# Attention output with its layer norm tile by tile, its weights loaded in the prologue, and the last feed-forward chunk moved into the tail block

## The reference

```python
x = _layernorm(x + _L0_attn_ref(x, ...))   # 16 heads of 64, full 2048x2048 softmax, rope; out @ out_w + out_b
x = _layernorm(x + _L0_ffn_ref(x, ...))    # two layers: windowed attention (8 heads, window 64) + GEGLU
x = _layernorm(x + _L1_attn_ref(x, ...))   # rwkv: five token-shift mixes, a decaying scan over the tokens, gate
x = _layernorm(x + _L1_ffn_ref(x, ...))    # silu(x @ wg) * (x @ wu) @ wd, weights given as integers
```

```python
return out @ out_w + out_b                     # end of _L0_attn_ref
def _layernorm(x): return (x - mean(x)) / sqrt(var(x) + 1e-5)
# end of each of the two layers of _L0_ffn_ref (HID = 341):
h = shift_token(x); h = (h - mu) / sqrt(var + 1e-5) * lg + lb
h = h @ w1 + b1
a, g = split(h, 2);  h = a * gelu(g, exact)
x = x + h @ w2 + b2
# the scan of _L1_attn_ref
S = exp(w_t)[..., None] * S + k_t[..., :, None] * v_t[..., None, :]
```

## Time and profile before

| | us |
|---|---|
| median of 3 runs | 1880.84 (1878.97 to 1882.34) |
| profiled execution | 1881.02 |
| span of the profiled execution | 1879.2 |
| mean granted TensorE clock | 0.971 of full speed |
| heads end, attention output begins | 1234.3 |
| next block after the norm (`local_layers`) begins | 1295.9 |
| first instruction of `phase_tail` | 1691.6 |

### The profile page before, as it was taken

The page is one execution under the profiler, slowest core; times in us unless marked ns, Lnnn a source line. Parts: engine busy times, 40 slices in busy tenths (PEclk is TensorE's granted clock), DMA queues, the critical chain, the costliest instruction groups (busy, mean ns, idle before and its releaser), DMA issues. The chain is left out here.

```text
span 1879.2 us, 54358 instructions
## 1 busy us (share of the span) xinstructions
PE 1753.0 (93%) x23048; PEld 1111.1 (59%) x23048; DVE 1409.3 (75%) x2595; ACT 1417.4 (75%) x1780; POOL 1426.3 (76%) x846
## 2 busy tenths in 40 slices
PE   5899999999999999999999999985899999977997
PEld 2466666666666666666666666674556666653454
DVE  5778778787878778787878776425988888844785
ACT  1688888888888888888888889922898888843463
POOL 3599999999998998999999999974765666624122
PEclk8899999999999999999999999987999999997988
DMA  4011010101111010101111010050211111100000
GB/s 121 24 25 31 19 31 22 28 23 30 24 25 27 22 31 19 31 23 26 27 26 27 19 27 2 2 174 12 44 42 36 36 37 40 34 7 13 0 1 23
DMA packets 71082, 56.91 MB, mean 30 GB/s; under 512 B 29197, under 2 KB 64185, under 8 KB 70841
## 3 DMA queue, kind: packets, MB, share of 16 engines
q1 hardware_dynamic: 70840, 53.44, 11.3%
HBM read 14.54 MB, written 1.05 MB: 8 GB/s over the span
## 5 line engine op out<-in xcount | busy, mean ns | idle before, releaser
L294 POOL TENSOR_TENSOR ah_probs_lo<-ah_probs,ah_probs_hi 128x1024 f16<-128x1024 f32 x512 | 1074.8, 2135 | 107.1 <-ACT ah_probs L493 104.8
L550 DVE TENSOR_REDUCE ah_part_max<-ah_p_m 128x1 f32<-128x512 f32 x1024 | 666.8, 684 | 165.4 <-PE ah_p_m L358 156.0
L490 ACT ACTIVATE ah_probs_hi<-ah_p_s 128x1024 f16<-128x1024 f32 x512 | 529.0, 1033 | 183.3 <-PE ah_p_s L377 177.4
L493 ACT ACTIVATE ah_probs<-ah_p_s 128x1024 f32<-128x1024 f32 x512 | 529.8, 1035 | 0.0
L391 PE MATMUL ah_p_o<-ah_v_hi,ah_probs_hi 128*128 128x65 f16 x4096 | 470.6, 195 | 4.9 <-POOL ah_probs_lo L294 4.7
L393 PE MATMUL ah_p_o<-ah_v_lo,ah_probs_hi 128*128 128x64 f16 x4096 | 470.5, 193 | 0.0
L395 PE MATMUL ah_p_o<-ah_v_hi,ah_probs_lo 128*128 128x65 f16 x4096 | 470.3, 194 | 0.0
L391 PEld LDWEIGHTS ah_p_o<-ah_v_hi,ah_probs_hi 128*128 128x128 f16 x4096 | 383.1, 98 | 86.0 <-DVE a_attn L565 12.2
L393 PEld LDWEIGHTS ah_p_o<-ah_v_lo,ah_probs_hi 128*128 128x128 f16 x4096 | 378.5, 98 | 91.5
L358 PE MATMUL ah_p_m<-ah_k_hi_lo,ah_q_hi_twice 128*128 128x512 f16 x1024 | 393.9, 385 | 7.0 <-DVE ah_part_max L550 5.5
L376 PE MATMUL ah_p_s<-ah_q_hi_twice,ah_k_hi_lo 128*128 128x512 f16 x1024 | 388.7, 380 | 1.1 <-ACT ah_probs L493 0.9
(11 more groups left out here) (291 smaller groups left out, 3096.1 us busy)
## 6 DMA issues: line engine op xcount, KB each, us to landing
ba_v_skew<-ba_v_own SPq DMA_DIRECT2D x64, 129.0 KB, 2.3
ah_q_hi_twice<-ah_hi SPq DMA_DIRECT2D x128, 64.0 KB, 2.0
ah_k_hi_lo<-ah_hi SPq DMA_DIRECT2D x64, 64.0 KB, 1.9
ah_one_k_hi<-ah_hi SPq DMA_DIRECT2D x64, 64.0 KB, 2.0
ah_k_hi_lo<-ah_lo SPq DMA_DIRECT2D x64, 64.0 KB, 2.0
ah_max_q_lo<-ah_lo SPq DMA_DIRECT2D x64, 64.0 KB, 2.0
ah_w_head<-in_w_heads SPq DMA_DIRECT2D x16, 160.0 KB, 2.4
bw_rot<-in_rot SPq DMA_DIRECT2D x4, 512.0 KB, 9.9
```

The costliest lines, as they stand in the source:

```text
L294: pool.tensor_tensor(pl[:, p % RW, :, :], pb[:, p % RP, :, :], ph[:, p % RW, :, :], ALU.subtract).then_inc(lo_pool, 1)
L490: act.activation(ph[:, p % RW, :, :], p_s[:, p % 2, :, :], ACT.Exp, scale=HD ** -0.5)
L493: act.activation(pb[:, p % RP, :, :], p_s[:, p % 2, :, :], ACT.Exp, scale=HD ** -0.5).then_inc(exp_done, 1)
L550: dve.tensor_reduce(part[:, t, 2 * half + b:2 * half + b + 1], p_m[:, b, :], AX, ALU.max).then_inc(maxed, 1)
```

## The change

It has three parts.

**Attention output.** `wo`, the output bias and the value bias are loaded in the prologue of `mha_heads`, behind the weights of head 1. There PE multiplies the value bias with `wo` (eight products between two pieces of the prologue), DVE adds the output bias, and POOL adds the result to x in place before its loop. In `mha_out` nothing is left of this path. The row is written back into x, and its statistics and aggregate follow on DVE at once. Of each group of four tiles the root (ACT), the reciprocal and shift (DVE) and the norms (all on ACT, four tiles) are done during the next group; the last group's follow the last tile. `layernorm_block` is gone. `wqkv` is held only for this block.

**Last chunk.** `w1`, `w2`, `b1` and `h2T` are kept over the end of `local_layers`, whose pipeline now ends three steps earlier, after the last `h2T`. In `phase_tail` PE begins with the six products, then `turn_x(0)`, the twelve products back, and `turn_x(1)`. ACT has the three gelus ahead of `norm(0, 0)`, DVE the three multiplications between the statistics of chunks 0 and 1, and the residual behind `delta_z(0)`.

**Scan state.** The state is kept in two chunk buffers per head instead of four, with a copy of one column after the scan in the first three chunks.

```diff
@@ mha_heads: SP, POOL, PE, DVE
+                sp.dma_start(bo[:, :, :], a["b_o"]).then_inc(wo_in, 16)
+                sp.dma_start(bv[:, :], a["b_v"]).then_inc(wo_in, 16)
+                sp.dma_start(wo[:, :, :], a["wo_a"].rearrange("(c p) d -> p c d", p=P)).then_inc(wo_in, 16)
...
+                pool.wait_ge(x_turned, NCH)
+                pool.wait_ge(bias_done, 1)
+                pool.tensor_tensor(x_sb[:, :, :], x_sb[:, :, :], bias[:, :, :].to_broadcast([P, NT, D]),
+                                   ALU.add).then_inc(biased, 1)
...
+                pe.wait_ge(wo_in, 3 * 16)
+                for c in range(IC):
+                    mm = pe.matmul(p_a[:, 0:D], bv[:, c:c + 1].to_broadcast([P, P]), wo[:, c, :], start=(c == 0),
+                                   stop=(c == IC - 1))
+                mm.then_inc(bias_turned, 1)
                 early_v(LEAD_G - 2)
                 for q in range(PAIRS_A):
                     maxima(q)
+                pe.wait_ge(bias_done, 1)
                 turn_max(0)
...
                 low(LEAD_G - 2)
+                dve.wait_ge(bias_turned, 1)
+                dve.tensor_tensor(bias[:, 0, :], p_a[:, 0:D], bo[:, 0, :], ALU.add).then_inc(bias_done, 1)
                 low_v(LEAD_G - 2)
@@ mha_out: ACT, POOL, DVE
+                def root(g):
+                    act.wait_ge(var_done, TPC * (g + 1))
+                    act.activation(std[:, g * TPC:(g + 1) * TPC], mv[:, g * TPC:(g + 1) * TPC, 1], ACT.Sqrt,
+                                   bias=eps[:, 0:1]).then_inc(std_done, 1)
+
+                def norm(g):
+                    act.wait_ge(shift_done, g + 1)
+                    for t in range(g * TPC, (g + 1) * TPC):
+                        act.activation(x_sb[:, t, :], x_sb[:, t, :], ACT.Identity, scale=rstd[:, t:t + 1],
+                                       bias=shift[:, t:t + 1]).then_inc(normed, 1)
+
+                act.wait_ge(eps_set, 1)
+                act.activation(std[:, 0:1], eps[:, :], ACT.Sqrt).then_inc(table_in, 1)
+                act.wait_ge(table_in, 1)
                 for t in range(NT):
                     act.wait_ge(turned, t + 1)
                     if t >= 2:
                         act.wait_ge(y_ready, t - 1)
                     act.activation(aT[:, t % 2, 0:4, :], p_t[:, t % 2, 0, :].rearrange("p (c t) -> p c t", t=P),
                                    ACT.Copy).then_inc(copied_a, 1)
+                    g, i = divmod(t, TPC)
+                    if i == 2 and g >= 1:
+                        root(g - 1)
+                    if i == 3 and g >= 1:
+                        norm(g - 1)
+                root(NT // TPC - 1)
+                norm(NT // TPC - 1)
 
             @block.gpsimd
             def _(pool):
-                pool.wait_ge(w_in, 48)
-                pool.tensor_copy(bvw[:, :, :], bv[:, :].unsqueeze(2).to_broadcast([P, IC, P])).then_inc(widened, 1)
-                pool.wait_ge(bias_done, 1)
-                pool.tensor_tensor(xb[:, :, :], x_sb[:, :, :], bias[:, :, :].to_broadcast([P, NT, D]),
-                                   ALU.add).then_inc(biased, 1)
                 local.prepare(pool)
 
             @block.vector
             def _(dve):
+                def row(t):
+                    dve.wait_ge(y_ready, t + 1)
+                    dve.tensor_tensor(x_sb[:, t, :], p_y[:, t % 2, 0:D], x_sb[:, t, :], ALU.add).then_inc(rows_ready, 1)
+                    dve.wait_ge(rows_ready, t + 1)
+                    dve.bn_stats(stats[:, t, :], x_sb[:, t, :]).then_inc(stats_done, 1)
+                    dve.wait_ge(stats_done, t + 1)
+                    dve.bn_aggr(mv[:, t, :], stats[:, t, :]).then_inc(var_done, 1)
+
+                def shifts(g):
+                    ts = slice(g * TPC, (g + 1) * TPC)
+                    dve.wait_ge(std_done, g + 1)
+                    dve.reciprocal(rstd[:, ts], std[:, ts]).then_inc(rstd_done, 1)
+                    dve.wait_ge(rstd_done, g + 1)
+                    dve.scalar_tensor_tensor(shift[:, ts], mv[:, ts, 0], -1.0, rstd[:, ts], ALU.mult,
+                                             ALU.mult).then_inc(shift_done, 1)
+
+                dve.memset(eps[:, :], LN_EPS).then_inc(eps_set, 1)
                 for t in range(NT):
-                    if t == 1:
-                        dve.wait_ge(bias_turned, 1)
-                        dve.tensor_tensor(bias[:, 0, :], p_b[:, 0:D], bo[:, 0, :], ALU.add).then_inc(bias_done, 1)
                     dve.wait_ge(turned, t + 1)
                     if t >= 2:
                         dve.wait_ge(y_ready, t - 1)
                     dve.tensor_copy(aT[:, t % 2, 4:8, :],
                                     p_t[:, t % 2, 1, :].rearrange("p (c t) -> p c t", t=P)).then_inc(copied_b, 1)
-                    if t == 1:
-                        dve.wait_ge(biased, 1)
                     if t >= 1:
-                        dve.wait_ge(y_ready, t)
-                        dve.tensor_tensor(rows[:, t - 1, :], p_y[:, (t - 1) % 2, 0:D], xb[:, t - 1, :],
-                                          ALU.add).then_inc(rows_ready, 1)
-                dve.wait_ge(y_ready, NT)
-                dve.tensor_tensor(rows[:, NT - 1, :], p_y[:, (NT - 1) % 2, 0:D], xb[:, NT - 1, :],
-                                  ALU.add).then_inc(rows_ready, 1)
-        layernorm_block(nc, ln, "aln_", rows, x_sb)
+                        row(t - 1)
+                    g, i = divmod(t, TPC)
+                    if i == 3 and g >= 1:
+                        shifts(g - 1)
+                row(NT - 1)
+                shifts(NT // TPC - 1)
@@ local_layers
-STEPS_B = TILES + FIRST_G - 1
+STEPS_B = TILES + 6
...
-            return (m, r) if 0 <= m < CHUNKS else (m, -1)
+            return (m, r) if 0 <= m < CHUNKS - 1 else (m, -1)
@@ phase_tail: PE, ACT, POOL, DVE
+                        if n == 1:
+                            pe.wait_ge(lres_done, 1)
...
+                def last_products():
+                    for banks, col, ready in ((last_gate, lw.hid, lgate_ready), (last_value, 0, lvalue_ready)):
+                        for k, (first_row, n) in enumerate(chunks):
+                            cs = slice(col + first_row, col + first_row + n)
+                            pe.matmul(banks[k][0:n, :], lw.w1[:, DEPTH - 1, cs], lw.hT2[:, 1, :], start=True,
+                                      stop=True).then_inc(ready, 1)
+
+                def last_down():
+                    pe.wait_ge(lhidden, len(chunks))
+                    for t in range(TPC):
+                        for k, (first_row, n) in enumerate(chunks):
+                            n += k == len(chunks) - 1
+                            mm = pe.matmul(p_kr[:, 1, t * P:(t + 1) * P], hT[0:n, 1, k, t * P:(t + 1) * P],
+                                           lw.w2[0:n, DEPTH - 1, k, :], start=(k == 0), stop=(k == len(chunks) - 1))
+                    mm.then_inc(ldown_ready, 1)
+
+                last_products()
                 turn_x(0)
+                last_down()
                 turn_x(1)
...
+                for k, (first_row, n) in enumerate(chunks):
+                    act.wait_ge(lgate_ready, k + 1)
+                    act.activation(hT[0:n, 0, k, :], last_gate[k][0:n, :], ACT.Gelu,
+                                   bias=lw.b1[0:n, DEPTH - 1, 1, k:k + 1]).then_inc(gelu_done, 1)
                 norm(0, 0)
...
+                pool.memset(hT[:, 1, HC - 1, :], 1.0).then_inc(ones_set, 1)
                 pool.memset(neg_half[:, :], -0.5).then_inc(cleared, 1)
-                pool.memset(st[:, :, 0:1], 0.0).then_inc(cleared, 1)
+                pool.memset(st[:, :, 0, 0:1], 0.0).then_inc(cleared, 1)
...
                 dve.memset(xTp[:, 0:1], 0.0).then_inc(zeroed, 1)
+                dve.wait_ge(ones_set, 1)
+                for k, (first_row, n) in enumerate(chunks):
+                    dve.wait_ge(gelu_done, k + 1)
+                    dve.wait_ge(lvalue_ready, k + 1)
+                    dve.scalar_tensor_tensor(hT[0:n, 1, k, :], last_value[k][0:n, :],
+                                             lw.b1[0:n, DEPTH - 1, 0, k:k + 1], hT[0:n, 0, k, :], ALU.add,
+                                             ALU.mult).then_inc(lhidden, 1)
                 ln_stats(0, 1)
...
                 delta_z(0)
+                dve.wait_ge(ldown_ready, 1)
+                dve.tensor_tensor(x_sb[:, tiles(CLAST), :], each(p_kr[:, 1, :]), x_sb[:, tiles(CLAST), :],
+                                  ALU.add).then_inc(lres_done, 1)
                 ln_stats(0, 2)
                 delta_z(1)
...
                     if c == 0:
+                        dve.wait_ge(lres_done, 1)
                         ln_stats(0, CLAST)
...
-                        dve.wait_ge(scanned, n - HCH + 1)
-                    dve.tensor_tensor_scan(st[:, h, xtok(c)], dec[:, n % 2, :], kv[:, n % 2, :],
-                                           st[:, h, c * CH:c * CH + 1], ALU.mult, ALU.add).then_inc(scanned, 1)
```

(5 more changed lines are left out.)

117 lines of the change are left out of this document (37 added, 80 removed).

## The result

The changed kernel takes 1860.66 us (median of 5 runs, 1856.94 to 1865.37), the kernel before on the same chip 1882.06: ratio 0.9893, 95% interval 0.9876 to 0.9910. The medians differ by 21.4 us, the ratio stands for 20; 22.2 were forecast and the range held. The two profiled executions differ by 20.3 us of span (1879.2 and 1858.9), and milestones read from the timelines say where. Each is the start of an instruction: a turn, the last row's addition on VectorE, the first eight records of a `mixes` on PE, the last scan.

What follows compares the result with a forecast made beforehand. PE was taken as busy 93% of the span, so gains come only where it waits: attention output 10.9 plus last chunk 11.6 less scan state 0.3 is 22.2 us off 1881.02, giving 1858.8; range 1854.0 to 1867.0.

Steps and rivals of the forecast that it cites:

- Attention output, front: Start of attention output: without the bias path, turn 2 starts at about 1240.0 instead of 1246.88, gaining 6.9 us.
- Attention output, middle: Attention output's tiles: pitch stays 2.66 us, but shifts wait beside POOL's preparation, costing 1.0 us, bounds 0 and 3.
- a few tenths: Attention output, middle: room left for ACT's norms making the copy behind them late, given a slack of 0.1 us.
- the slack of 0.1 a group: Attention output, middle: ACT's copy behind the norms done about 3.4 us after PE's turns, asked for at 3.5.
- Attention output, end: After the last row's start: last norm ends after 3.5 us instead of 8.54, gaining 5.0, bounds 4.3 and 5.4.
- Prologue and carry: Heads' prologue: loads and bias work cost nothing, bounds -0.5 and +1; scan state's column copies: 0.3 us, bounds 0 and 1.8.
- Last chunk: Tail start: six products begin at 1679.9, mixes(0) at 1697.9 instead of 1707.53; gain 11.6 us by mixes(1).
- it stays: Tail: PE's clock stays full through the 2.0 to 2.2 us idle before turn_x(1); if it falls, gain 7.3.
- the first rival: Tail: the clock falls in the gap, last chunk gains 7.3 us instead of 11.6, time 1863.1; chance 0.28.
- DVE or ACT holds PE: Attention output: DVE steps wait for POOL or ACT's norms delay copies, 5.5 us in all, time 1864.3; chance 0.09.
- The slower case: Heads: new loads or bias path upset them, PE waiting longer for wo or turns losing 0.35 us; 1885 us; chance 0.04.

Runs made afterwards that it cites:

- filling: Changed kernel with extra identity transposes in PE's waits: last stage alone 1859.7 us; heads' end, last local turn, tail and last stage 1853.55 us.
- the one-input form: Changed kernel with each group's shift computed by four 128x1 instructions with one tensor input each, instead of one with two: 1860.68 us, ratio 0.9891.

## Why the prediction was right, point by point

The range held and the order of the waits was right. That the forecast came so close is in part luck: the moved parts gave 18.1 us, where 22.2 were forecast, and 2.2 came from stages that had been put at nothing.

- *Attention output, front* (6.9): 6.6. The clock came back 5 us after the start, as taken over from the bias product. That it is half at the start is not the block's doing but comes from short waits of PE at the heads' end, which I had not looked at; filling them brings 2.0 more.
- *Attention output, middle* (-1.0, bounds 0 and 3): -1.8 in the profile of the changed kernel, and -1.0 to -5.0 in the others of that form. The mechanism was right and its size too small: I took half an instruction of POOL for each of a group's two instructions. The reciprocal never waited (0.14 to 0.15), and the shift waited to the end of POOL's first, second or third. The bound of 3 was passed in two profiles, in one of them with 1.6 us of half clock. The share of ScalarE, "a few tenths", is 0.24: the slack of 0.1 a group was a lack of 0.12.
- *Attention output, end* (5.0): 5.3. The bounds for this whole part were added up wrongly: 8 to 12.5 is stated, its terms give 7.2 to 12.3. The measured 10.1 lies in both.
- *Prologue and carry* (0 and -0.3): 0 and -0.18, shown by the kernels that have the one without the other.
- *Last chunk* (11.6): 8.9 up to mixes(0), where 9.6 was forecast; the order of waits was right to the half microsecond. Of the missing 0.7, most is the six products: their pace of before was taken over, 7.0 us, and with more of them at half clock they took 8.0. The step that failed is the clock. I asked only whether it would fall in the gap ahead of turn_x(1), and took "it stays" from a wait of 2.41 us that had done no harm. It did stay there, and fell after the following gap of 2.22 us, when PE was at work again, and again after one of 2.53. That cost 1.3 to 1.4 in each of two `mixes` and left a gain of 8.1, between the forecast and the first rival's 7.3. Whether it falls is not a property of the code: the kernel with the last chunk alone ran the same mixes(1) at full pace (8.39 to mixes(2), 9.71 in the changed kernel). One difference is 0.2 off in the prediction: 13.5 less 2.2 is 11.3 and not 11.5; with a full clock 11.50 was measured.
- *What I left out*: the stages whose code doesn't change moved by -1.3 (local block) and +2.7 (last stage). The latter is the clock, shown by filling. For the former nothing was tested: 382 to 387 us over the thirteen profiles. The trace of the changed kernel puts it down to half clock too (0.8 us at the block's start, 0.7 at 1403), and what makes it fall there stays open. With the 0.85 of the heads these come to 2.2 us of gain that no term has.
- *Rivals*: "DVE or ACT holds PE" was priced at 5.5 through all DVE steps; only the shift waits, but that came to 3.9 and, with a fall of the clock, 5.0 in two profiles. (The prediction calls it "the third rival below"; it is the second.) The slower case had nothing for it.

The page "SBUF — State Buffer" of the Trainium skill, section "Who interferes with whom", was borne out on both sides: the two-input instruction waited up to 2.97 us beside POOL's work and the one-input form never. The conclusion that only `shifts` pays holds: rows and statistics stayed at 0.29 us. For the length of the wait the measurement goes further than one instruction of POOL: six of fourteen shifts let a second or a third one pass.
